# Dense experts started beside the router's softmax, with rows turned once, and another end of the recurrence

## The reference, cut to what matters

```python
x = x + 0.5 * _L1_ffn_ref(_layernorm(x), ...)   # causal attention, then 8 experts
x = x + _L1_attn_ref(_layernorm(x), ...)        # recurrence over the 512 tokens
x = x + 0.5 * _L1_ffn_ref(_layernorm(x), ...)   # the causal block again

# causal block, after attention gave a = o @ Wo + bo + x
h2 = _ln(a, ln2_g, ln2_b)
logits = h2 @ Wr + br
kmask = logits >= top_k(logits, 2)[0][..., -1:]
w = softmax(where(kmask, logits, -inf))
mid = gelu(einsum('bsd,edf->bsef', h2, e_w1) + e_b1)   # all 8 experts for all tokens
eo = einsum('bsef,efd->bsed', mid, e_w2) + e_b2
return einsum('bse,bsed->bsd', w, eo) + a

# recurrence, after the scan gave o, one row per token
out3 = stack([z, z, o], axis=2)      # two zero rows ahead of each row of o
out = out3.reshape(B, 3 * N, ...)[:, -N:]
gate = sigmoid(x @ Wo1 @ Wo2)
out = out * gate
out = (out - mean(out)) * rsqrt(var(out) + 1e-5) * ln_w
return out @ Wout
```

## Time and profile before

| | |
|---|---|
| three runs | 5418.72, 5418.9 and 5402.63 us, median 5418.72 |
| profiled execution | 5396.82 us, its span 5395.1 us |
| PE busy | 4310.9 us (80%) |
| DVE busy | 3364.5 us (62%) |
| ACT busy | 2538.4 us (47%) |
| POOL busy | 1781.8 us (33%) |
| chain that ended last | PE 57%, DVE 21%, POOL 8%, ACT 7%, issue 5%, DMA 1%, SPq 1% |
| granted TensorE clock, mean | 0.882 |

### The profile page before, as it was taken

The page is one execution under the profiler, slowest core; times in us unless marked ns, Lnnn a source line. Parts: engine busy times, 40 slices in busy tenths (PEclk is TensorE's granted clock), DMA queues, the critical chain, the costliest instruction groups (busy, mean ns, idle before and its releaser), DMA issues.

```text
span 5395.1 us, 115473 instructions
## 1 busy us (share of the span) xinstructions
PE 4310.9 (80%) x42948; PEld 2545.5 (47%) x42948; DVE 3364.5 (62%) x15488; ACT 2538.4 (47%) x4899; POOL 1781.8 (33%) x3632
## 2 busy tenths in 40 slices
PE   2789999999999999964699978748550069998999
PEld 2645555555555555533544446535330033445776
DVE  2187777777777777732177631799999966761111
ACT  1346777777777777731344534323220024553333
POOL 3155666666666666652132210000000012220000
PEclk9879999999999999976789979879775568997999
DMA  4500000000000000003301000010010000000000
GB/s 125 152 10 2 2 12 2 6 8 2 12 2 6 8 2 6 2 1 110 109 9 35 1 1 13 13 25 16 15 33 0 11 1 1 1 1 1 1 0 16
DMA packets 131566, 104.22 MB, mean 19 GB/s; under 512 B 21936, under 2 KB 110288, under 8 KB 131024
## 3 DMA queue, kind: packets, MB, share of 16 engines
q1 hardware_dynamic: 126928, 88.67, 6.0%
q0 software_dynamic: 4096, 8.40, 0.5%
HBM read 74.56 MB, written 22.48 MB: 18 GB/s over the span
## 4 chain that ended last, share of the span: by engine, by line
PE 57%; DVE 21%; POOL 8%; ACT 7%; issue 5%; DMA 1%; SPq 1%; POOLq 0%; DVEq 0%; ACTq 0%
PE ps L1296 5%; PE ps L1336 4%; PE ps L1281 4%; PE ps L1481 4%; PE ps L1620 4%; PE ps L1610 4%; PE ps L1493 4%; PE ps L1257 3%; PE ps L1267 3%; DVE arena L2823 2%; PE ps L1522 2%; DVE arena L2843 2%; PE ps L1166 2%; ACT arena L1921 2%; ACT arena L1903 2%
## 5 line engine op out<-in xcount | busy, mean ns | idle before, releaser
L2281 DVE CUSTOM_DVE_ANT_0 arena<-ps,mask_win 128x256 f32<-128x256 f32 (+1 forms) x3072 | 1008.3, 385 | 251.8 <-PE ps L1281 250.7
L1903 ACT ACTIVATE arena<-ps 128x512 f32<-128x512 f32 (+1 forms) x1536 | 751.5, 543 | 557.7 <-PE ps L1296 555.1
L1296 PE MATMUL ps<-arena 32*64 32x384 f32 (+2 forms) x6144 | 740.4, 476 | 72.8 <-ACT arena L1903 72.4
L1281 PE MATMUL ps<-arena 32*64 32x192 f32 (+2 forms) x12288 | 692.8, 323 | 14.4 <-DVE arena L2281 13.9
L2454 DVE CUSTOM_DVE_ANT_0 arena<-ps,mask_cau 128x512 f32<-128x512 f32 (+3 forms) x1024 | 447.0, 487 | 264.2 <-PE ps L1481 261.2
L2020 ACT ACTIVATE arena<-ps 128x512 f32<-128x512 f32 (+2 forms) x768 | 362.9, 526 | 448.3 <-PE ps L1493 448.1
L964 POOL TENSOR_SCALAR_AFFINE_SELECT arena<-arena 128x1024 f32<-128x1024 f32 x384 | 419.8, 1093 | 388.6 <-ACT arena L1903 385.9
L1281 PEld LDWEIGHTS ps<-arena 32*64 32x64 f32 x12288 | 379.2, 133 | 269.5 <-DVE arena L2281 95.9
L1493 PE MATMUL ps<-arena 32*128 32x512 f32 (+2 forms) x1536 | 482.4, 615 | 25.5 <-ACT arena L2020 25.5
L1481 PE MATMUL ps<-arena 32*128 32x512 f32 (+3 forms) x2048 | 419.8, 514 | 19.7 <-DVE arena L2454 15.7
L1166 PE MATMUL ps<-ident,arena 128*128 128x128 f32 x944 | 174.8, 316 | 292.8 <-DMA arena<-xs 120.5
(11 more groups left out here) (333 smaller groups left out, 8833.0 us busy)
## 6 DMA issues: line engine op xcount, KB each, us to landing
w<-in_L_w_dram SPq DMA_DIRECT2D x160, 256.0 KB, 3.2
arena<-xs SPq DMA_DIRECT2D x10, 512.0 KB, 6.8
ys<-arena SPq DMA_DIRECT2D x10, 512.0 KB, 4.4
xs<-zero SPq DMA_DIRECT2D x1, 2560.0 KB, 11.2
w<-in_L_w_dram SPq DMA_DIRECT2D x1, 2048.0 KB
scr_k<-arena SPq DMA_DIRECT2D x8, 256.0 KB, 2.3
scr_v<-arena SPq DMA_DIRECT2D x8, 256.0 KB, 2.9
scr_f<-arena SPq DMA_DIRECT2D x8, 256.0 KB, 3.2
```

Of the source, the lines that this page charges most:

```text
L1281: m = pe.matmul(ps[64 * h:64 * h + 64, bank, s.at(v) + lo:s.at(v) + hi], Q[p][r][rows, v, q0:q0 + 64], K[p][r][rows, s.k0 + lo:s.k0 + hi], ...
L1296: m = pe.matmul(out[64 * h:64 * h + 64, :, lo:hi], K[p][r][rows, t.k0 + lo:t.k0 + lo + 64], Q[p][r][rows, 0:2, t.q0 + lo:t.q0 + hi], start ...
L1903: act.activation(PTs[m % L.SLOTS][:, k * w:(k + 1) * w], bank[:, 0:w], exp, scale=-1.0)\
L2281: x = dve.tensor_tensor_reduce(out=seen, in0=bank[:, s.at(v):s.at(v) + s.kw], in1=mask, scale=1.0, scalar=NO_SCORE, op0=ALU.add, op1=ALU.m ...
```

## The change

- The loops and the function `expert_main` go; one function `dense(use)` on TensorE and ScalarE, and `add` on VectorE, serve both causal blocks in straight-line code. The barriers before and after the router go, as do those at the end.
- ScalarE's copies of the turned rows in `expert_pre` go to HT, which holds all 32 tiles, over A. `dense` reads its rows there (in four pieces, where groups go by time), so only C is turned per group; the first turn of C comes after seven steps. `post_share` is put ahead of the bias of H, since HT overwrites A. The recurrence's KW moves behind HT, and its normalised rows go to the two buffers zT (as HR).
- The bias sum is added after expert 3 instead of 1.
- The end of the recurrence: GpSimd scales Wout by ln_w and clears EX during the recurrence, and TensorE makes `shift`, the sum of Wout's rows. After the barrier VectorE writes gated results to EX at once. TensorE turns EX to rows of tokens; VectorE takes statistics there; GpSimd makes roots in two parts (8 and 24 columns). TensorE multiplies unnormalised rows with Wout, and the results are scaled: batches 0 and 1 by VectorE, straight into X, batches 2 to 7 by ScalarE, into A. `centred` adds the mean's share, `shift` times minus mean times root, and takes the statistics for the next block: for batches 0 and 1 at once, for the others inside the second attention, where `summed` stands in the first. GpSimd's roots for these go there too.
- X is stored by eight DMAs, each when its batch is done.

```diff
 class ExpertPhase:
+    def tile(self, use, g, i):
+        return TPB * g + i if use else TPB * (TPB * (g % 2) + i) + g // 2
...
+        HT = take(TILES * P)
         KW = [take(CH, 2, HD) for _ in range(2)]
+        HR = [z.rearrange("p (i k) -> p i k", k=P) for z in zT]
...
-            for k in range(3):
-                barrier(sp, PH_CAUSAL2 + k)
-            sp.dma_start(out.rearrange("b (i p) f -> p (b i) f", p=P), X[:]).then_inc(stored, 16)
+            for b in range(BATCHES):
+                sp.wait_ge(moe.acc_done, moe.result(1, b, EXPERTS - 1) + 2 + START)
+                sp.dma_start(out.rearrange("b (i p) f -> p b i f", p=P)[:, b], X[:, TPB * b:TPB * (b + 1), :])\
+                    .then_inc(stored, 16)
...
 pool
+                pool.wait_ge(loaded, LAST_LOADED)
+                pool.tensor_tensor(pos[:, 3, :], pos[:, 3, :], fcol[:, 0:1].broadcast_to([P, P]), ALU.mult)
+                pool.wait_ge(R.kt_ready, R.GROUPS // 2)
+                pool.wait_ge(R.step, R.CHUNK * (R.GROUPS // 2 - 1) + 1)
+                pool.memset(EX, 0.0).then_inc(R.cleared, 1)
+            def gated_roots():
+                for k, (at, n) in enumerate(((0, 2 * TPB), (2 * TPB, TILES - 2 * TPB))):
+                    nb = r1[:, at:at + n]
+                    pool.wait_ge(R.rows_var, BATCHES if k else 2)
+                    chain.link(newton_rows(n, at))
+                    chain.link(pool.tensor_tensor(nb, mv[:, at:at + n, 0], rstd[:, at:at + n], ALU.mult))
+                    pool.tensor_scalar(nb, nb, -1.0, None, ALU.mult).then_inc(R.rows_rstd, 1)
...
-                roots(2, 0, 2)
-                roots(2, 2, BATCHES - 2)
+            gated_roots()
+            roots(2, 0, 2)
+            attention(cau, BATCHES)
...
 tensor, dense(use)
                 def turn(g):
-                    pe.wait_ge(yb_ev, g + START)
-                    pe.wait_ge(S.T_ev, g + START)
+                    pe.wait_ge(yb_ev, S.group(use, g) + START)
+                    pe.wait_ge(S.c_ready, use + 1)
                     for i in range(TPB):
-                        pe.transpose(ps[0:EXPERTS, 7, i * P:(i + 1) * P], C[:, R.tile(g, i), :], ident[:])
-                    for i in range(TPB):
-                        m = pe.transpose(ps[:, 5, i * P:(i + 1) * P], H[:, R.tile(g, i), :], ident[:])
+                        m = pe.transpose(ps[0:EXPERTS, 7, i * P:(i + 1) * P], C[:, S.tile(use, g, i), :], ident[:])
                     m.then_inc(S.T_done, 1)
+                def rows(g):
+                    if use:
+                        return HT[:, TPB * P * g:TPB * P * (g + 1)]
+                    return HT.rearrange("p (b j t) -> p j b t", j=TPB, t=P)[:, g // 2, TPB * (g % 2):TPB * (g % 2 + 1)]
-                        if s == 2:
+                        if s == 7 and g == 0:
+                            turn(g)
+                        if s == 9:
                             biases(g)
...
+            pe.wait_ge(R.ex_ready, 1)
+            for b0 in (0, 4):
+                for b in range(b0, b0 + 4):
+                    gated_rows(b)     # b >= 4 waits for rows_var; four transposes
+                for b in range(b0, b0 + 4):
+                    gated_out(b)      # 4, 5 wait for x_done, 6, 7 for z_ev; four products
+            pe.wait_ge(R.z_ev, BATCHES - 2)
...
 scalar
+            act.wait_ge(R.rows_rstd, 2)
+            for b in range(2, BATCHES):
+                act.wait_ge(R.y_done, b + 1)
+                for i in range(TPB):
+                    t = TPB * b + i
+                    m = act.activation(A[:, t, :], ps[:, 4 + b % 4, i * P:(i + 1) * P], ACT.Identity,
+                                       bias=zero[:, 0:1], scale=rstd[:, t:t + 1])
+                m.then_inc(R.z_ev, 1)
...
 vector
                 def post_bias(b):
+                    post_share(b)
                     x = tiles(H, b)
                     dve.tensor_tensor(x, x, row(crow[:, 3, :]), ALU.add).then_inc(h_ready, 1)
-                    post_share(b)
+            def centred(b):
+                if b < 2:
+                    dve.wait_ge(R.x_done, b + 1)
+                else:
+                    dve.wait_ge(R.z_ev, b - 1)
+                    chain.link(dve.tensor_tensor(tiles(X, b), tiles(A, b), tiles(X, b), ALU.add))
+                for t in range(TPB * b, TPB * (b + 1)):
+                    chain.add(dve.scalar_tensor_tensor(out=X[:, t, :], in0=shift, scalar=r1[:, t:t + 1],
+                                                       in1=X[:, t, :], op0=ALU.mult, op1=ALU.add))
+                chain.join()
+                entry_stats(b)
...
+            dve.wait_ge(R.cleared, 1)
+            dve.tensor_tensor(EX[:, :, 1::3], OF[:, :, SEEN - OUT:], GATE, ALU.mult).then_inc(R.ex_ready, 1)
+            for b in range(BATCHES):
+                gated_stats(b)        # statistics of the turned rows, from PSUM
+            for b in range(2):
+                dve.wait_ge(R.rows_rstd, 1)
+                dve.wait_ge(R.y_done, b + 1)
+                for i in range(TPB):
+                    t = TPB * b + i
+                    m = dve.scalar_tensor_tensor(out=X[:, t, :], in0=ps[:, 4 + b % 4, i * P:(i + 1) * P],
+                                                 scalar=rstd[:, t:t + 1], in1=X[:, t, :], op0=ALU.mult, op1=ALU.add)
+                m.then_inc(R.x_done, 1)
+                centred(b)
```

More of the change, by code:

```diff
@@ L10 @@
-from contextlib import ExitStack, contextmanager
+from contextlib import ExitStack
 import numpy as np
@@ L80, in link @@
         self.join()
[L83 to L108, removed]
 class ScoreItem:
@@ L812, in _ @@
             load(fcol[:, 0:1], d["rec_lnw"].rearrange("(p a) -> p a", a=1))
-            sp.wait_ge(loaded, n[0])
-            for k in range(2):
-                barrier(sp, PH_CAUSAL1 + k)
+            assert n[0] == LAST_LOADED
             def group_out(g):
@@ L1027, in attention @@
                 rsqrt(TPB)
-            def expert_main(S, v0):
-                def rows(b, p):
-                    pool.tensor_copy(Cs[p], tiles(C, b))
-                    pool.tensor_copy(zs[p], tiles(S.src, b)).then_inc(S.x_ready, 1)
-                rows(0, 0)
-                rows(1, 1)
-                with counted_loop(pool, "pool moe", BATCHES // 2 - 1, (chain, norms)) as it:
-                    for p in range(2):
-                        b = 2 * it + p
-                        pool.wait_ge(S.T_done, v0 + b + 1 + START)
-                        gate(pool)
-                        rows(b + 2, p)
             def routing_constants(use):
@@ L1724, in _, with dense @@
             routed_experts(1)
[L1726 removed]
+            def dense(use):
                 S = moe
@@ L1835, in _ @@
-            pe.wait_ge(R.ex_ready, 1)
-            for b in range(BATCHES):
-                if b >= 2:
-                    pe.wait_ge(R.x_done, b - 1)
-                for i in range(TPB):
-                    m = pe.matmul(ps[:, b % 2, i * P:(i + 1) * P], EX[:, b, i * P:(i + 1) * P], pos[:, 3, :],
+                if use:
+                    down(S.GROUPS - 1, *order[-1])
+            attention(cau, 0, 0)
+            expert_pre(2 * BATCHES)
+            dense(0)
+            pe.wait_ge(R.w_ready, 1)
@@ L1846, in _ @@
+            expert_pre(3 * BATCHES)
+            dense(1)
         @block.scalar
@@ L2054, in attention @@
                 heads_turned(shared_use("oT", m0, BATCHES - 1, after=True))
-            def expert_main(S, v0, b1):
-                E = S.experts
-                def turn(b, p):
-                    act.wait_ge(S.T_done, v0 + b + 1 + START)
-                    if S is moe:
-                        act.activation(cT[p][0:EXPERTS, :], ps[0:EXPERTS, 6, :], copy)
-                    act.activation(zT[p], ps[:, 5, :], copy).then_inc(S.T_ev, 1)
-                def stage(b, p, first=False, last=False):
-                    for e in range(E):
-                        for c in range(CHUNKS):
-                            act.wait_ge(S.up_done, ((v0 + b) * E + e) * CHUNKS + c + 1)
-                            act.activation(hid[c % 2], ps[:, c % 2, :], gelu, bias=b1(e)[:, c:c + 1])\
-                                .then_inc(S.gelu_done, 1)
-                            if (e, c) == (0, 1) and not last:
-                                turn(b + 1, 1 - p)
-                turn(0, 0)
-                run_batches(act, "act experts", (), stage)
             def expert_pre(v0):
@@ L2889, in newton @@
+                centred(b)
+            attention(cau, BATCHES, SHARED_PER_RUN)
+            expert_pre(3 * BATCHES, False)
+            for g in range(moe.GROUPS):
+                for e in range(EXPERTS):
+                    add(1, g, e)
 def newton(eng, chain, y, w, t):
```

367 lines of the change are left out of this document (126 added, 241 removed).

## The result

The changed kernel takes 5365.7 us (median of 6 runs, 5356.9 to 5376.7), the kernel before beside it 5419.9 (5402.6 to 5432.0): ratio 0.9915, 95% interval 0.9895 to 0.9935. That is 54 us less by the medians, where 66 us less were forecast on the profiled execution. The change went the way on which 0.90 was laid; 5365.7 lies inside the whole range (5314 to 5380), but outside the forecast's own (5325 to 5362). The two profiled executions differ by only 30.6 us (spans 5395.1 and 5364.5).

The account below looks back on a forecast made before the run. The prediction saw three places where the chain stands still though work is at hand, with VectorE's recurrence steps and TensorE's products setting the pace elsewhere. Terms summed to −66.3 us, applied to the 5409.3 mean: 5343, range 5314 to 5380.

Parts of the forecast that it names:

- first seam, to the first product: After the first attention: turns start without a barrier and the first expert product precedes the softmax's end; −22.4 us.
- recurrence's end: From gated product to the second attention's first turn: a new chain of 39.6 us replaces 60.9; −21.3 us.
- second attention: Centring of batches 2 to 7 moves beside it, on VectorE and GpSimd; +5 us, bounds 0 and +30.
- 1 us charged per GELU: At each seam: the first GELU stands behind ScalarE's exponential; 1 us charged, bounds 0 and 6 at the first.
- the rival of a fast router: Router stretches run at 2.4 GHz, as no pause precedes them; products 7 us earlier each, 5329 us; chance 0.10.
- a last stage at the low clock: Rival: dense stages, opening without a pause, stay at 1.2 GHz; 5460 us at 64 steps; chance 0.05.
- the first attention carries nearly this: Second attention: the first attention's similar work, 507.3 against 502.9 us, gave 4.4 us as the added work's price.
- gaps from VectorE's and GpSimd's added work: Rival, second attention: added work holds TensorE up and the granted clock falls; +30 us, 5373; chance 0.14.
- The sign set against the forecast: The forecast is wrong if granted clock falls below 0.8 for long in the second attention or last stage.
- The rule set against the change: Second attention: two-input VectorE operations and reading GpSimd operations exclude one another; +27 us if all thirty moved operations meet one.
- The bias sum's later place: Dense stages: adding it at expert 3 delays TensorE's turn of C, but more than ten steps stand between; nothing.
- the rival without a gain at the recurrence's end: Roots and ScalarE's six batches, one after another, fill the 60.9 us again; +21 us, 5364; chance 0.08.

Follow-up runs that it names:

- e2: Changed kernel with the router's turns at both seams waiting until all eight batches' rows are there; 5391.9 us, ratio 0.9948.
- e3: Changed kernel with the first expert product of both dense stages waiting for the experts' shares C; 5382.6 us, ratio 0.9931.
- e4: Changed kernel with batches 2 to 7 centred, and their roots taken, before the second attention instead of beside it; 5364.9 us, ratio 0.9896.
- e9: Changed kernel with VectorE's centring of batches 2 to 7 before the second attention, GpSimd's roots still beside it; 5377.3 us, ratio 0.9908.
- f1: Changed kernel with e6's edits and the bias sum back at its earlier place in every group but the first; 5349.0 us, ratio 0.9881.
- g1: f1 with the sharing of the attention's result put back behind its bias; 5357.5 us, ratio 0.9891.
- e6: Changed kernel with the output weights' column mean taken off once, so no mean's share is added to X; 5358.7 us, ratio 0.9871.
- e1: The changed kernel again, no edit, for a second profile; 5372.9 us, ratio 0.991.
- e0: The kernel before again, no edit, for a second profile; 5431.5 us in its one run.
- e7: Changed kernel with TensorE given products nobody reads, from 36 steps before the recurrence's end until the second attention; 5555.2 us, ratio 1.0233.

## Why the prediction was right, and where it was not

The means of the table's first three and of its next two rows, set against the forecast's terms (us):

| term | forecast | by the profiles |
|---|---|---|
| first seam, to the first product | −22.4 | −22.4 (45.2 to 22.8) |
| first dense stage and recurrence | +0.6 | +2.3 (1082.7 to 1085.0) |
| recurrence's end | −21.3 | −24.1 (63.3 to 39.3) |
| second attention | +5 | +14.3 (503.8 to 518.1) |
| second seam, to the first product | −20.9 | −21.3 (43.9 to 22.6) |
| last stage | −1.6 | −2.0 (467.3 to 465.3) |
| tail | −5.7 | −6.7 (10.6 to 3.9) |
| all that the change touches | −66.3 | −59.9 |
| to the first attention, and that | 0 | +7.6 (3199.4 to 3207.0) |

(The 1 us charged per GELU stands in the second and the sixth term.)

- *Seams.* Right in mechanism and size, and about three quarters of the first gain and more of the second put back by halves (e2, e3). The router's stretch stayed at a granted clock of 0.50, as taken, so the rival of a fast router did not come; nor did that of a last stage at the low clock, which had 1.00 from 4895.8 on. The charge for the GELU was 1; TensorE waited 0.41 for it in the first stage (e3's timeline shows the same 0.41) and 0.26 in the last.
- *Recurrence's end.* Right by the chain; no run puts the old end back. It came out 2 us shorter than worked out; the chain that ended last was the one through VectorE's two batches and GpSimd's double root, ready for the normalisation at 4348.7, and not ScalarE's six batches, which were done at 4345.6.
- *Second attention.* This is the term that was mis-sized: 14.3, not 5. The step that failed is "the first attention carries nearly this", from which 4.4 was read as the price. That difference took the shortest of three first attentions (507.3, 517.2, 525.0) against a second that hardly varies (502.9 to 504.3); from the mean of the three it would have been 12.7 and not 4.4. e4 and e9 price it by itself: 12 to 13 us. The mechanism of the rival, gaps from VectorE's and GpSimd's added work, holds at about half of its 30 us. By the granted clock of the traces the stage spent 143 us at 0.50 in the changed kernel, 127 in e4 and 120 in e9: half of the 16 us between the first two, an estimate of 8 out of the 12, can be the clock's, and the longer wait for VectorE's maxima accounts for the other 4; in e9 it is waiting alone. The sign set against the forecast, a clock below 0.8 for long in this stage, tells little: the kernel before has about 121 to 125 us at 0.50 there.
- The rule set against the change had its price here too, and a small one. Of the 24 scaled additions moved beside the attention one met it, at 1.06 us: the first of four that stood behind a mask selection of 1.63 us (from 4398.74). The timeline of VectorE for these four and the next:

```profile
4399.45 1.85 DVE L2477 SCALAR_TENSOR_TENSOR X<-arena,r,X 128x128 f32<-128x128 f32 x4
...
4405.36 1.14 DVE L2477 SCALAR_TENSOR_TENSOR X<-arena,r,X 128x128 f32<-128x128 f32 x4
```

  The 24 together took 9.0 us, 0.7 more than at their median of 346 ns. The Trainium skill, "SBUF — State Buffer", "SBUF: two separate sides", says that a VectorE operation with two SBUF inputs and a GpSimd operation that reads SBUF exclude one another for a whole instruction; the trace agrees in that one case. The 27 us that count a meeting for every operation are far off.
- *Recurrence.* The bias sum's later place was costed at nothing, because more than ten steps stood between. It costs 3 to 4.5 us: it makes VectorE wait longer for ScalarE's projected rows (f1 and g1 against e6).
- *The baseline.* The sum was made on a quick execution (5396.8) and applied to the mean of four times, 5409. The kernel before, measured beside each of the changed ones, has medians of 5416.0 to 5425.7, and 5419.9 beside the first: 5420 − 66 is 5354, and 5420 − 60 is 5360. So of the 23 us between 5343 and 5366 some 11 are the baseline and 6 the terms; the remaining 6 lie within the chance of the first attention and what stands before it. By its time alone the result sits at the rival without a gain at the recurrence's end (5364), which did not happen: that the terms add up so near is also luck, as 9 us too few for the second attention were made good in part by 3 and 1 at the recurrence's end and the tail.

## What to carry to other kernels

Filling a pause with work that is already there (a seam with a barrier in it) was worth its full length here, and could be read off the chain of waits to within 1 us. Work moved beside a stage counts as hidden only where a run shows it: here what was moved behind VectorE and GpSimd came back at its full price, because both stand in TensorE's loop. And before terms are taken from the difference of two stages in one profile, a second profile should show how far the same stage varies by itself.

## What the runs showed of the hardware

The same instructions took 507 to 528 us, and longer the longer the granted clock was at 0.50 among them (108 to 160 us). In the five executions compared instruction by instruction (two of before; changed, e1, e3) VectorE's times agree within about 1 us up to 90 us into the first attention; then the clock falls for 7 us (before), not at all (e0), or for 20 (the other three). A busy TensorE was no guard: over the seams it was busy 22.2 of 23.0 us at 0.50. And feeding it before a stage held the clock at 1.00 only up to the stage's opening: TensorE stood 4.1 us for VectorE there, and the clock was at 0.50 from 0.6 us after it went on (e7).
